# Attention loop: phases 0 and 1 of each chunk are multiplied with V in one block on TensorE, ahead of score tile 8

## The chip, the core and the metric

The kernel runs on one core of one Trainium2 chip. The metric is the device time of one execution in microseconds, median of several runs. The engines work from queues of their own and meet at semaphores: TensorE (PE, with its weight loads as PEld), VectorE (DVE), ScalarE (ACT), GpSimd (POOL) and SyncE (SP), which here only starts DMAs.

## What is computed

A gated cross-attention block and a mixture of experts, for 16 batches of 224 rows of width 512, with 750 context rows each:

```python
x = x + tanh(g_xattn) * xattn(layernorm(x), ctx, ctx, ctxb, ...)
x = x + tanh(g_ffn) * ffn(layernorm(x), ...)

# xattn, 16 heads of 32
Q, K, V = q_x @ Wq + bq, k_x @ Wk + bk, v_x @ Wv + bv        # split by head
scores = einsum('bhqd,bhkd->bhqk', Q, K) / sqrt(32)
scores = scores * gate[:, None, None, :]                     # from ctxb, 0.1 or 1
attn = softmax(scores)
out = einsum('bhqk,bhkd->bhqd', attn, V) ... @ Wo + bo
```

All is float32. The change touches the attention only.

## The kernel before

The attention is a loop over batches, with the first and the last batch written out of the same function `batch` and 14 passes of a loop between them. Each engine has its own order, written by hand. There is no scheduler: what stands ahead in an engine's code stands ahead in its queue.

A batch has four **chunks** c of four heads. A chunk has 12 **ticks** u = 0 to 11: in each, `score_columns` (L1155) makes one transposed score tile of 125 keys by 224 queries, twice, for one head, into one of two PSUM buffers `st`, and ScalarE's `exponential` (L613) turns it into `probs_t`. Tile u may be written once exponential u − 2 is done. Four ticks are a **phase**: phase 0 is ticks 0 to 3, phase 1 ticks 4 to 7, phase 2 ticks 8 to 11. `probs_t` holds two phases, so that exponential 8 needs phase 0 to have been read.

`attend(b, c, p)` (L1172) multiplies phase p with V: eight matmuls into the four 32-column strips of the array, a **block**. In the trace each shows as two records, so a block is x16. It waits for the last exponential of its phase, for p = 0 also for `normed`: VectorE's `normalize_output` of the chunk before, which reads and frees the tile `pv` and writes `out_t` (L869 to L871). `sum_up` (L1181) adds the sums of the exponentials behind phase 2, in the same 32-column form.

Between the ticks TensorE does other work:
- `next_scores(b, h, t)` (L1129), a score row of a head that comes 6 heads later, into the single tile `score`. Each needs VectorE's maximum (L848) of the row before. From h = 16 on it is a head of the next batch, and (16, 0), behind tile 6 of chunk 2, needs the stacked keys k_stack of that batch.
- `turn_shift` (L1143), a small transposition of the maxima, which ScalarE copies (L621), VectorE splits and ScalarE's DMA (L638) places in q_stack for the next chunk's or batch's tiles.
- the projections: V of the current and the next batch (L1103), K (L1093) and Q (L1081) of the next, the output projection of the last (L1116). They share three PSUM tiles `proj`; each is taken when its reader of three projections ago is done. The second half of Q takes the one that VectorE reads for q_lo (L831).

The keys of the next batch go this way: a half (K0a, K0b, ...) is projected on TensorE; VectorE gates it (`fresh`, L843); ScalarE makes the high part (`k_hi`, L583); GpSimd the low part (`k_lo`, L437); SyncE stores both (L301) and loads the stack (L317). In GpSimd's queue of chunk 1 the low part of K0b stands behind two additions (L482, L484) that need exponentials 8 and 9. In ScalarE's queue of chunk 1, `place_shift` (two DMA issues) and a normalisation (L602) stand between exponentials 8 and 9, and of chunk 2 the copy k_hi of K2a stands ahead of exponential 7.

V of the next batch goes from `proj` to `v_sb` by ScalarE's `copy_values` (L590). In chunk 3 ScalarE's code has:

```python
exponential(b, 3, u)
...
if not last and u == 6:
    copy_values(n, 0, b)        # n = b + 1
```

and `copy_values` waits until the old V tile has been read:

```python
act.wait_ge(pv_done, phases(n - 1, DC - 1, kt // 2) + 1)
```

which for tile 0 is phase 0 of chunk 3. Exponential 7 stands behind this copy.

## Time and profile before

| | |
|---|---|
| runs | 2049.89 us (2047.63 to 2052.6), 3 runs |
| profiled execution | 2065.15 us, its span 2063.2 |
| TensorE busy | 1948.6 us, 94% of the span |
| GpSimd, VectorE, ScalarE busy | 59%, 54%, 38% |
| attention loop | from about 78 to 1480 us, 15 batches of 88 us, the last 80 |
| granted TensorE clock | 0.969 over the span; 1.00 from 104 to 1421 us |

A share of busy time is an average; where an engine's queue is followed from record to record, the start of one to the start of the next is what it cost. A record of TensorE can overlap the next one. "[0.19 <-DVE out_t L871]" at a row's end is time without work ahead of it and what ended it. The rows below are mostly from the batch that begins at 694.45 us.

### The profile page before, as it was taken

The numbers are of one execution on the slowest core, as the hardware profiler recorded it, in microseconds if no ns is written. First come the engines' busy times: TensorE is split into PE (matmuls) and PEld (weight loads), VectorE is DVE, ScalarE is ACT, GpSimd is POOL, SyncE is SP. The second block draws the span as 40 slices with busy tenths as digits, with TensorE's granted clock in tenths as the row PEclk, the third lists the DMA queues.
The fourth block names the chain that finished last, engine by engine and source line by source line (L and its number), as shares of the span: only waits on it lengthen the run. The fifth ranks groups of instructions, "written<-read, shape, count | busy, mean of one in ns | idle before, by whom it ended". The sixth has DMA issues, their size and how long they took to land. (4 is left out here: it accounts for less than half of the span.)

```text
span 2063.2 us, 40622 instructions
## 1 busy us (share of the span) xinstructions
PE 1948.6 (94%) x12484; PEld 1510.4 (73%) x12485; DVE 1117.1 (54%) x1772; ACT 777.1 (38%) x1541; POOL 1226.6 (59%) x1391
## 2 busy tenths in 40 slices
PE   6799999999999999999999999998769999999899
PEld 5587877878777787877878777785458666666687
DVE  4565565655556555565665656555347333333576
ACT  3335444444544444444444544444222122221000
POOL 2367677776767777677776767766524333333352
PEclk9899999999999999999999999998579999999899
DMA  7754837457383654837557383664062554445675
GB/s 221 187 144 120 240 98 203 137 148 202 107 234 102 183 161 121 246 98 194 143 141 206 109 227 112 173 170 131 19 248 77 179 165 146 149 144 172 178 222 152
DMA packets 170571, 330.51 MB, mean 160 GB/s; under 512 B 20295, under 2 KB 69447, under 8 KB 169879
## 3 DMA queue, kind: packets, MB, share of 16 engines
q1 hardware_dynamic: 156700, 286.97, 49.3%
q0 software_dynamic: 10880, 33.56, 6.0%
q10 hardware_dynamic: 2944, 9.38, 1.2%
q8 instruction: 27, 0.44, 0.1%
q14 instruction: 20, 0.16, 0.0%
HBM read 214.17 MB, written 115.14 MB: 160 GB/s over the span
## 5 line engine op out<-in xcount | busy, mean ns | idle before, releaser
L848 DVE TENSOR_REDUCE neg_max<-score 112x1 f32<-112x750 f32 x512 | 480.7, 939 | 570.4 <-PE score L1129 569.3
L613 ACT ACTIVATE probs_t<-st 125x448 f32<-125x448 f32 x768 | 413.6, 542 | 514.9 <-PE st L1155 512.1
L482 POOL TENSOR_TENSOR acc<-acc,probs_t 125x448 f32<-125x448 f32 x256 | 309.5, 1209 | 66.1 <-ACT probs_t L613 64.3
L1155 PE MATMUL st<-q_stack,k_stack 98*125 98x224 f32 x1536 | 336.1, 302 | 5.0 <-ACT probs_t L613 2.7
L1093 PE MATMUL proj<-ctx_hi,weights 128*128 128x376 f32 (+1 forms) x1024 | 329.7, 347 | 0.0
L1155 PEld LDWEIGHTS st<-q_stack,k_stack 98*125 98x125 f32 x1536 | 269.0, 192 | 60.1 <-issue 28.3
L484 POOL TENSOR_TENSOR acc<-acc,probs_t 125x448 f32<-125x448 f32 x256 | 299.0, 1168 | 20.1
L1129 PE MATMUL score<-k_stack,q_stack 96*112 96x512 f32 (+1 forms) x1024 | 286.1, 361 | 23.8 <-DMA k_stack<-k_parts 12.4
L1103 PE MATMUL proj<-weights,ctx_hi 128*125 128x512 f32 x768 | 249.1, 406 | 5.0 <-issue 5.0
L474 POOL TENSOR_TENSOR acc<-probs_t 125x448 f32<-125x448 f32 x128 | 146.1, 1143 | 168.3 <-PE pv L1181 149.7
L1129 PEld LDWEIGHTS score<-k_stack,q_stack 96*112 96x112 f32 x1024 | 160.5, 179 | 80.7 <-issue 53.5
L1093 PEld LDWEIGHTS proj<-ctx_hi,weights 128*128 128x128 f32 x1024 | 192.4, 190 | 25.3 <-issue 16.1
L1172 PE MATMUL pv<-probs_t,v_sb 125*32 125x224 f32 x3072 | 191.9, 369 | 7.4 <-DVE out_t L871 6.6
L437 POOL TENSOR_TENSOR k_lo<-fresh,k_hi 128x376 fp32r<-128x376 f32 (+1 forms) x128 | 117.1, 915 | 97.3 <-ACT k_hi L583 97.3
L1093 PE MATMUL proj<-parts,weights 128*128 128x376 f32 (+1 forms) x512 | 172.1, 336 | 0.0
L2229 PE MATMUL gu_ps<-gu_sb,xg_t 128*128 x576 | 155.4, 398 | 4.0 <-DVE xg_t L2181 1.7
L2229 PEld LDWEIGHTS gu_ps<-gu_sb,xg_t 128*128 128x128 f32 x576 | 99.0, 191 | 78.4 <-issue 66.4
L1103 PE MATMUL proj<-weights,parts 128*125 128x512 f32 x384 | 152.5, 397 | 0.0
L1103 PEld LDWEIGHTS proj<-weights,ctx_hi 128*125 128x125 f32 x768 | 125.7, 189 | 34.6 <-issue 16.1
L1081 PE MATMUL proj<-xn_t,wq_sb 128*128 128x224 f32 x512 | 122.3, 364 | 12.4 <-DVE q_lo L831 10.3
L1116 PE MATMUL proj<-wo_sb,out_t 128*112 128x512 f32 x256 | 126.0, 607 | 0.0
L1172 PEld LDWEIGHTS pv<-probs_t,v_sb 125*32 125x32 f32 x3072 | 82.8, 111 | 55.9 <-DVE out_t L871 10.0
(212 smaller groups left out, 2758.3 us busy)
## 6 DMA issues: line engine op xcount, KB each, us to landing
k_stack<-k_parts SPq DMA_DIRECT2D x192, 375.0 KB, 6.2
ctx_raw<-in_ctx_t SPq DMA_DIRECT2D x64, 375.0 KB, 10.0
k_parts<-k_hi SPq DMA_DIRECT2D x64, 375.0 KB, 6.9
k_parts<-k_lo SPq DMA_DIRECT2D x64, 375.0 KB, 7.2
y_slots<-y_sb SPq DMA_DIRECT2D x72, 256.0 KB, 3.0
q_stack<-q_parts SPq DMA_DIRECT2D x64, 224.0 KB, 5.9
gu_sb<-in_w_gu ACTq DMA_DIRECT2D x4, 2048.0 KB, 15.6
x_in<-in_x SPq DMA_DIRECT2D x16, 448.0 KB, 9.2
```

Source lines behind the costliest of these rows:

```text
L474: nc.gpsimd.tensor_tensor(acc[0:KW, 2 * pair:2 * pair + 2, :], tiles(c, 0, pair, 0), tiles(c, 0, pair, 1), ALU.add).then_inc(added, 1)
L482: nc.gpsimd.tensor_tensor(both, both, tiles(c, p, pair, 0), ALU.add).then_inc(half_added, 1)
L484: nc.gpsimd.tensor_tensor(both, both, tiles(c, p, pair, 1), ALU.add).then_inc(added, 1)
L613: act.activation(probs_t[0:KW, (c * PHASES + p) % 2, u % HC, :], st[u % 2][0:KW, 0:2 * L], ACT.Exp)\
L848: nc.vector.tensor_reduce(neg_max[:, h // HC % 2, h % HC, t:t + 1], score[0:QW, 0:S], axis=AX.X, op=ALU.max, negate=True).then_inc(maxed, 1)
L1093: ins = nc.tensor.matmul(bank[:, 0:w], wp[:, d, c * P:(c + 1) * P], xp[:, d, at:at + w], start=(d == 0 and k == 0), stop=(d == DC - 1 and ...
L1103: ins = nc.tensor.matmul(bank[0:KW, :], xp[:, d, kt * KW:(kt + 1) * KW], wp[:, d, :], start=(d == 0 and k == 0), stop=(d == DC - 1 and k = ...
L1116: ins = nc.tensor.matmul(bank[0:QW, :], out_t[:, c, t * QW:(t + 1) * QW], wo_sb[:, c, :], start=(c == 0), stop=(c == DC - 1))
L1129: ins = nc.tensor.matmul(score[0:QW, at:at + w], q_stack[0:ROWS, h, t * QW:(t + 1) * QW], k_stack[0:ROWS, h, at:at + w], start=True, stop= ...
L1155: ins = nc.tensor.matmul(st[u % 2][0:KW, k * L:(k + 1) * L], k_stack[0:SHIFTED, h, kt * KW:(kt + 1) * KW], q_stack[0:SHIFTED, h, :], start ...
L1172: ins = nc.tensor.matmul(pv[j * DH:(j + 1) * DH, 0:L], v_sb[0:KW, kt, at:at + DH], probs_t[0:KW, (c * PHASES + p) % 2, j, k * L:(k + 1) * ...
L2229: ins = nc.tensor.matmul(gu_ps[k % 2][:, 0:GATE_UP], xg_t[:, k % 2, c, :], gu_sb[:, bass.ds(expert, 1), c, :].rearrange("p a m -> p (a m)" ...
```

## The change

In each chunk `attend` of phase 0 moves from behind tile 7 to directly ahead of tile 8, and `attend` of phase 1 from behind tile 10 to directly behind it. Phase 2 stays behind tile 3 of the next chunk. Nothing else is changed: no other engine's code, no buffer, no semaphore. The diff, cut to chunk 0 and chunk 3 (chunks 1 and 2 are changed in the same way; in chunk 2 there is no `turn_shift` ahead of the block, the score row (16, 1) stands there):

```diff
                 score_columns(b, 0, 7)
-                attend(b, 0, 0)
                 if not first:
                     project_out(b - 1, 0, b, (2, 3))
                 next_scores(b, 8, 1)
                 turn_shift(b, 1, b)
+                attend(b, 0, 0)
+                attend(b, 0, 1)
                 score_columns(b, 0, 8)
...
                 score_columns(b, 0, 10)
-                attend(b, 0, 1)
                 next_scores(b, 9, 1)
...
                 score_columns(b, 3, 7)
-                attend(b, 3, 0)
                 if not last:
                     project_v(1, b, (2, 3))
                 next_scores(b, 20, 1)
                 if not last:
                     turn_shift(n, 0, b)
+                attend(b, 3, 0)
+                attend(b, 3, 1)
                 score_columns(b, 3, 8)
...
                 score_columns(b, 3, 10)
-                attend(b, 3, 1)
                 if not last:
                     project_v(2, b, (2, 3))
```

What TensorE's queue holds in chunk 3 of the loop, from tile 7 to tile 8, before (st are tiles, pv blocks, proj with weights V projections, score a score row in two halves):

```order
L1155 MATMUL st<-q_stack,k_stack 125x224 x2
L1172 MATMUL pv<-probs_t,v_sb 32x224 x8
L1103 MATMUL proj<-weights,ctx_hi 125x512 x2
L1103 MATMUL proj<-weights,parts 125x512
L1126 REGISTER_ALU
L1129 MATMUL score<-k_stack,q_stack 112x512
L1129 MATMUL score<-k_stack,q_stack 112x238
L1043 REGISTER_ALU
L1143 MATMUL proj<-ident,neg_max 8x112
L1151 REGISTER_ALU
L1155 MATMUL st<-q_stack,k_stack 125x224 x2
```

and now:

```order
L1155 MATMUL st<-q_stack,k_stack 125x224 x2
L1103 MATMUL proj<-weights,ctx_hi 125x512 x2
L1103 MATMUL proj<-weights,parts 125x512
L1126 REGISTER_ALU
L1129 MATMUL score<-k_stack,q_stack 112x512
L1129 MATMUL score<-k_stack,q_stack 112x238
L1043 REGISTER_ALU
L1143 MATMUL proj<-ident,neg_max 8x112
L1172 MATMUL pv<-probs_t,v_sb 32x224 x8
L1167 REGISTER_ALU
L1172 MATMUL pv<-probs_t,v_sb 32x224 x8
L1151 REGISTER_ALU
```

The first block stands behind the transposition L1143 instead of directly behind tile 7, and the second, which stood behind tile 10, directly behind the first. In chunk 1 of the loop, TensorE's queue behind the transposition, now:

```order
L1143 MATMUL proj<-ident,neg_max 8x112
L1172 MATMUL pv<-probs_t,v_sb 32x224 x8
L1167 REGISTER_ALU
L1172 MATMUL pv<-probs_t,v_sb 32x224 x8
L1151 REGISTER_ALU
L1155 MATMUL st<-q_stack,k_stack 125x224 x2
L1093 MATMUL proj<-ctx_hi,weights 128x374
L1093 MATMUL proj<-parts,weights 128x374
L1093 MATMUL proj<-ctx_hi,weights 128x374
L1081 MATMUL proj<-xn_t,wq_sb 128x224 x2
L1155 MATMUL st<-q_stack,k_stack 125x224 x2
```

Both blocks stand ahead of tile 8, of the end of the K0b projection (L1093) and of the first two query projections (L1081); before, only the first block stood ahead of them, further up. The other four engines' queues are the same as before.

## Rows read from the trace of the kernel before

**Rows 1.** Waits of TensorE, whole run: engine line <- whom, us in total, times, longest

```profile
PE score L1129 <- DMA k_stack<-k_parts: 12.4, 15, 3.3
```

**Rows 2.** TensorE timeline, chunk 3: start, us, engine, line, operation, tiles, count

```profile
770.13 0.38 PE L1155 MATMUL st<-q_stack,k_stack 98*125 98x224 f32 x2
770.35 0.50 PE L1129 MATMUL score<-k_stack,q_stack 96*112 96x512 f32 x2
770.69 0.63 PE L1103 MATMUL proj<-weights,ctx_hi 128*125 128x512 f32 x2
...
771.38 0.37 PE L1155 MATMUL st<-q_stack,k_stack 98*125 98x224 f32 x2
771.69 0.96 PE L1172 MATMUL pv<-probs_t,v_sb 125*32 125x224 f32 x16
772.58 0.73 PE L1103 MATMUL proj<-weights,ctx_hi 128*125 128x512 f32 x2
...
773.38 0.50 PE L1129 MATMUL score<-k_stack,q_stack 96*112 96x512 f32 x2
...
773.75 0.46 PE L1155 MATMUL st<-q_stack,k_stack 98*125 98x224 f32 x2
774.04 0.63 PE L1103 MATMUL proj<-weights,ctx_hi 128*125 128x512 f32 x2
```

**Rows 3.** TensorE timeline, chunk 2: a block with the sums behind it

```profile
742.64 0.96 PE L1172 MATMUL pv<-probs_t,v_sb 125*32 125x224 f32 x16
743.42 0.56 PE L1181 MATMUL pv<-acc,ones_col 125*32 125x224 f32 x8
```

**Rows 4.** ScalarE timeline, chunk 3: the V copy and exponential 7

```profile
772.72 0.60 ACT L590 ACTIVATE v_sb<-proj 125x512 f32<-125x512 f32 x1 [1.55 <-PE pv L1172]
773.21 0.54 ACT L613 ACTIVATE probs_t<-st 125x448 f32<-125x448 f32 x1
```

**Rows 5.** TensorE timeline, chunk 1

```profile
727.18 0.38 PE L1155 MATMUL st<-q_stack,k_stack 98*125 98x224 f32 x2
727.74 0.96 PE L1172 MATMUL pv<-probs_t,v_sb 125*32 125x224 f32 x16 [0.19 <-DVE out_t L871]
...
729.25 0.50 PE L1129 MATMUL score<-k_stack,q_stack 96*112 96x512 f32 x2
...
730.13 0.46 PE L1155 MATMUL st<-q_stack,k_stack 98*125 98x224 f32 x2
...
731.80 1.02 PE L1081 MATMUL proj<-xn_t,wq_sb 128*128 128x224 f32 x4 [0.69 <-DVE q_lo L831]
```

**Rows 6.** VectorE timeline, chunks 0 and 1: the maxima behind out_t

```profile
706.65 0.94 DVE L848 TENSOR_REDUCE neg_max<-score 112x1 f32<-112x750 f32 x1
...
727.60 0.93 DVE L848 TENSOR_REDUCE neg_max<-score 112x1 f32<-112x750 f32 x1
```

**Rows 7.** ScalarE timeline, chunk 1: exponentials 8 and 9

```profile
731.05 0.52 ACT L613 ACTIVATE probs_t<-st 125x448 f32<-125x448 f32 x1
...
733.28 0.52 ACT L613 ACTIVATE probs_t<-st 125x448 f32<-125x448 f32 x1
```

**Rows 8.** GpSimd timeline, chunk 1: low part of K0b

```profile
736.30 0.98 POOL L437 TENSOR_TENSOR k_lo<-fresh,k_hi 128x374 fp32r<-128x374 f32 x1
```

**Rows 9.** TensorE timeline, chunk 2 of two batches: first score row of next batch

```profile
573.31 0.59 PE L1129 MATMUL score<-k_stack,q_stack 96*112 96x512 f32 x2 [1.18 <-DMA k_stack<-k_parts]
...
749.91 0.59 PE L1129 MATMUL score<-k_stack,q_stack 96*112 96x512 f32 x2 [0.74 <-DMA k_stack<-k_parts]
```

**Rows 10.** ScalarE timeline, chunk 2: exponential 7 behind a key copy

```profile
752.60 0.53 ACT L613 ACTIVATE probs_t<-st 125x448 f32<-125x448 f32 x1
```

**Rows 11.** TensorE timeline, chunk 0: tile 7

```profile
706.45 0.38 PE L1155 MATMUL st<-q_stack,k_stack 98*125 98x224 f32 x2
```

**Rows 12.** Stretches of the last batch: us, busy by engine, PEclk, DMA share, GB/s

```profile
1421.00:1431.60 10.60, 6.35 (x52) 4.27 (x50) 8.26 (x14) 7.28 (x12) 6.97 (x13) 1.00 0.14 44
1431.70:1469.00 37.30, 30.29 (x179) 19.35 (x179) 16.82 (x20) 15.34 (x31) 25.18 (x19) 0.50 0.10 30
```

More of the change, by code:

```diff
@@ L1316, in batch @@
                 score_columns(b, 1, 7)
-                attend(b, 1, 0)
                 if not last:
@@ L1323, in batch @@
                 turn_shift(b, 2, b)
+                attend(b, 1, 0)
+                attend(b, 1, 1)
                 score_columns(b, 1, 8)
@@ L1332, in batch @@
                 score_columns(b, 1, 10)
-                attend(b, 1, 1)
                 if not last:
@@ L1374, in batch @@
                 score_columns(b, 2, 7)
-                attend(b, 2, 0)
                 if not last:
@@ L1378, in batch @@
                 next_scores(b, 16, 1)
+                attend(b, 2, 0)
+                attend(b, 2, 1)
                 score_columns(b, 2, 8)
@@ L1389, in batch @@
                 score_columns(b, 2, 10)
-                attend(b, 2, 1)
                 if not last:
```

## The prediction

> **What bounds the kernel now.** I read the waits first. TensorE's longest waits inside the loop are those for the stacked keys (k_stack), 12.4 us over 15 times [rows 1]. Then the timelines of one pass of the loop (694.4 to 782.7 us, 88.3 us; the passes repeat to within some tens of ns, except for the k_stack wait). TensorE's records follow each other without a gap, so whatever adds or removes time in its queue counts in full, and a delay elsewhere counts only where TensorE meets it. So I take the four chunks one by one, and ask at each new place of a block whether its data are there. I call the block of eight matmuls of a phase p0 or p1 and count score tiles 0 to 11 of a chunk.
>
> **What a visit to the 32-column form costs.** In chunk 3, a tile followed by a score row takes 0.22 us (770.13 to 770.35), but tile 7, followed by a block, takes 0.31 (771.38 to 771.69); the three projection records after the block take 0.80 (772.58 to 773.38) where the same three take 0.69 elsewhere (770.69 to 771.38); and the block takes 0.89 (771.69 to 772.58) [rows 2]. A block followed by the sums, which have the same form, takes 0.78 [rows 3]. So a visit costs 0.09 in, 0.11 out and about 0.10 in the group behind it. Merging removes one visit, 0.30 us. In chunks 0, 1 and 3 the block now stands behind the small transposition L1143, which already makes the tile behind it take 0.29 (773.75 to 774.04) instead of 0.22; there both old visits' entries and exits go and one exit stays, 0.48 us saved: two entries of 0.09, two groups behind of 0.10, one exit of 0.11, less 0.02 because the tile behind the merged block takes 0.31, not 0.29. How a block starts directly behind L1143 isn't shown: between 0 and 0.09 (the entry from a tile); I take 0.04. In sum the switches give back 0.44 us in each of three chunks and 0.30 in chunk 2, 1.6 us a batch. The Trainium skill (TensorEngine Tiling (Array Packing), Key Properties) says that changing the tiling mode drains TensorE. The rows agree, with the prices above; by this rule alone the change is a gain (that is rival B).
>
> **Chunk 3: a wait in a ring.** ScalarE's queue has, in this order, exponential 6, the copy of V tile 0 of the next batch, exponential 7. The copy may not overwrite V before p0 of chunk 3 has read it: it starts at 772.72, 1.03 us after the block's start at 771.69, exponential 7 starts 0.49 later and takes 0.54 [rows 2, 4]. Today p1 comes far later. Now p1 follows p0 at once and needs exponential 7. From tile 7 (time 0): tile 0.22, projection 0.69, score row and L1143 0.37 (773.38 to 773.75), so p0 starts at 1.28 and p1 could start at 2.06. Exponential 7 ends at 1.28 + 1.03 + 0.49 + 0.54 = 3.34; with 0.07 for the handover (block's end 772.65 to copy 772.72) p1 starts at 3.41. That is a **new wait of 1.35 us**. p1 takes 0.89, tile 8 starts at 4.30; today at 2.37 (773.75 − 771.38). At its old place p1 goes with 0.09 + 0.89 + 0.10 = 1.08. Net 4.30 − 2.37 − 1.08 + 0.02 + 0.04 = **+0.91 us**. Behind the waiting block in TensorE's queue stand tile 8 and all that follows; ScalarE and VectorE idle behind it.
>
> **Chunk 1: one wait for another, and the keys later.** Today p0 waits for VectorE's out_t (tile 7 at 727.18, block at 727.74: 0.56 instead of 0.30). It now stands later and that wait goes, 0.26. But the score row behind it, which p0 covered, needs VectorE's maximum that starts at 727.60 and takes 0.93: it ends 1.35 after tile 7, with handover 1.42, while TensorE is there at 0.22 + 0.52 = 0.74. New wait 0.68. (Score row, three key projections and L1143 take 0.88, 729.25 to 730.13; less 0.37 for the first and last as in chunk 3, three key projections take 0.51 to 0.52.) Behind the wait come these 0.88, the blocks 0.78 + 0.89: tile 8 starts at 3.97, today at 2.95 (730.13): +1.02 [rows 5, 6]. Then the q_lo wait in front of the query projection (0.69, [rows 5]) disappears, since VectorE is earlier and TensorE later; and p1's old place gives 1.08 back. So TensorE is, after chunk 1, 0.74 us ahead of today. But exponential 8 waits for tile 8. It starts today at 731.05, 3.87 after tile 7, held up by ScalarE's own queue; now not before 3.97 + 0.53 (tile 8's 0.46 and a handover) to 4.60: 0.63 to 0.73 later, I take 0.68. Exponential 9 follows 2.23 behind, bound by ScalarE's queue (two DMA issues, a normalisation) [rows 7]; GpSimd's two additions for phase 2 need it, and in its queue stands behind them the low part k_lo of K0b [rows 8], then the store, the load, and the first score row of the next batch in chunk 2, which already waits 0.74 here [rows 9]. So that row comes 0.68 (+0.04) later although TensorE is there 0.7 earlier: **+0.72 us**, and the k_stack wait grows from 0.8 to about 2.2. Bounds: 0.4 if ScalarE catches up, 0.9 if exponential 9 waits for tile 9.
>
> **Chunk 2.** All runs from that score row, T = 749.91. Exponential 7 stands in ScalarE's queue behind a key copy that needs VectorE's gated keys: it starts at 752.60, ends T + 3.23, so p1 can start at T + 3.30 [rows 9, 10]. TensorE would be there after a score row (0.34, up to 0.1 more behind a wait; I take 0.42), key projections 0.52, tile 0.22, key projections 0.52, score row 0.34, entry 0.09 and p0 0.78: 2.89. Wait 0.4, visit −0.30: **+0.10**, between −0.30 and +0.2.
>
> **Chunk 0.** The visits give 0.48 less 0.04, and the out_t wait of 0.07 goes. Score row (8,1) loses the cover of p0: VectorE's maximum starts at 706.65 and takes 0.94, so ends 1.14 after tile 7 (706.45) [rows 6, 11]; handed over at 1.21. TensorE has only tile 7 and one output projection to do until then, which no row of mine prices; if they take no less than 0.65 together the wait is at most 0.55, and if they take more than 1.21 it is nothing. I take a quarter of the way, 0.13, and as much for row (9,1), which loses the cover of p1: **−0.25**, between −0.55 and +0.2. No DMA, and no instruction of another engine's queue, is moved.
>
> **Sum.** −0.25 + 0.72 + 0.10 + 0.91 = 1.48 us for a full batch, 14 of them 20.7. The first batch has chunks 1 to 3 alike, 1.5. The last has no projections and no V copy or key chain; there the merge may save or cost 1, I take 0. In all **+22 us**: on the profiled execution's 2065.15 (span 2063.2 and 1.95 around it) 2087; on the median of the runs, 2049.89, the same 22, so 2072.
>
> **Rivals.** *A, forecast:* both the ring and the later keys, 2072. *B, the switches win:* the visits come out as worked out, the waits don't: if ScalarE's copy doesn't stand in the way (wait 1.35 gone) and the keys land early enough, a batch changes by −0.25 − 0.70 + 0.10 − 0.44 = −1.3, some 2031. It needs both: with the ring in place (+0.91) the rest would have to fall below −0.91, and even with the keys on time it is −0.85; the ring's wait decides, from 1.3 us downwards. Against it speaks the order of ScalarE's queue, in which the copy at 772.72 waited 1.55 us for the block and the exponential followed it [rows 4]. *C, the keys have slack in the timed runs:* they are 15 us faster than the profiled one, and 12.4 us of that could be this wait. Where the load isn't late, TensorE keeps its 0.70 and a batch comes to −0.25 − 0.70 + 0.10 + 0.91 = +0.06: 2051. Partial slack gives all between 2051 and 2072. *D, the clock:* over 1421 to 1431.6 us TensorE was busy 6.35 of 10.6 us, split by short waits, and behind it the granted clock is 0.50, the lower of its two levels (1.2 GHz) [rows 12]. A wait of 2.2 us (up to 2.7, where it is 1.2 today, 573.31 in [rows 9]) in each of 15 batches could do the same. If it falls after half of them and costs 1 to 3 us each, +7 to +22: 2079 to 2094. Against it: around that wait of 1.2 us the granted clock stayed 1.00. *E, nothing moves:* the order shows the blocks merged in TensorE's queue, so it could only be that gains and waits cancel, 2050.
>
> **How the numbers follow.** A 0.56, D 0.22, C 0.12 (half of it within 0.2%, which is about what a measurement of this kernel can tell from no change), B 0.08, E 0.02. Forecast 2072. Range: down to most of C, up to the greater part of D: 2054 to 2093. Slower by over 0.2% (above 2054): 0.56 + 0.22 + 0.06 = 0.84, with the edge of C 0.85; same 0.07; faster 0.08.
>
> **What would show it.** In chunk 3, p0 and p1 apart by some 2.1 us, ended by ScalarE's probs_t, 15 times; ScalarE's copy of V between them. In chunk 1, no wait for out_t and q_lo, one of 0.7 for neg_max. The first next-batch score row waiting 2.2 us for k_stack instead of 0.8. The granted clock 1.00 in the loop (A) or with gaps (D). The forecast is wrong if p1 doesn't wait in chunk 3, if the keys' low part isn't later behind tile 7, or if the merged block takes other than 1.67 us without a wait.

## The result, and the profile after

| | before | after |
|---|---|---|
| median of the runs | 2049.12 us, 4 runs | 2114.3 us, 4 runs (2104.96 to 2117.06) |
| profiled execution | 2065.15 us, span 2063.2 | 2113.91 us, span 2112.0 |
| a batch of the loop, mean of 14 | 88.23 us | 92.56 us |

After over before is 1.0321 (95% interval 1.0297 to 1.0346): 65 us slower. Forecast were 2072 and a range that ended at 2093, so the direction was right and the size too small by 42 us. The loop accounts for the result: 14 × 4.34 = 60.7 us. The two profiled spans differ by 48.8 us only, because the one before had 12 us more between the start of its last batch and its end (663.2 us against 651.1). So the predicted 1.48 us a batch stand against 4.34.

TensorE's waits after, over the whole run (engine line <- whom it waited for: us in total, times, longest), answer to [rows 1]:

```profile
PE score L1129 <- DMA k_stack<-k_parts: 32.4, 15, 4.7
PE score L1129 <- DVE neg_max L848: 20.8, 33, 3.3
PE pv L1172 <- ACT probs_t L613: 18.3, 17, 1.2
PE st L1155 <- DMA q_stack<-shift_rows: 17.6, 16, 2.6
PE pv L1172 <- DVE out_t L871: 1.9, 2, 1.4
```

Three of the four large ones were predicted: the keys (12.4 us before; one of the 15, 4.7 now and 3.3 then, lies ahead of the first batch at 55 us, and the 14 of the loop average 1.98 us, 1.64 to 2.57, against 0.65 before), the maxima, and ScalarE's exponential in chunk 3 (1.15 us, about once a batch). The fourth was not. L1155 is the score tile, and what it waits for is the placing of the maxima (`place_shift`) into q_stack.

**Chunk 3**, TensorE and then ScalarE (start, us, engine, line, operation, tiles, count, idle time before and what ended it), answers to [rows 2, 4]:

```profile
799.77 0.38 PE L1155 MATMUL st<-q_stack,k_stack 98*125 98x224 f32 x2
...
801.03 0.26 PE L1143 MATMUL proj<-ident,neg_max 112*8 112x112 f32 x1
801.22 0.96 PE L1172 MATMUL pv<-probs_t,v_sb 125*32 125x224 f32 x16
803.34 0.96 PE L1172 MATMUL pv<-probs_t,v_sb 125*32 125x224 f32 x16 [1.15 <-ACT probs_t L613]
804.23 0.48 PE L1155 MATMUL st<-q_stack,k_stack 98*125 98x224 f32 x2
```
```profile
802.25 0.60 ACT L590 ACTIVATE v_sb<-proj 125x512 f32<-125x512 f32 x1 [2.70 <-PE pv L1172]
802.75 0.54 ACT L613 ACTIVATE probs_t<-st 125x448 f32<-125x448 f32 x1
```

The ring stands there as worked out: block, copy of V, exponential 7, block. The blocks start 2.12 us apart, forecast was 2.13 (3.41 − 1.28). Tile 7 to tile 8 takes 4.46 us, forecast was 4.30.

**Chunk 1**, TensorE, then the exponentials 8 and 9, then GpSimd's low part of K0b, answers to [rows 5, 7, 8]:

```profile
752.49 0.38 PE L1155 MATMUL st<-q_stack,k_stack 98*125 98x224 f32 x2
...
753.90 0.59 PE L1129 MATMUL score<-k_stack,q_stack 96*112 96x512 f32 x2 [0.51 <-DVE neg_max L848]
...
754.85 0.26 PE L1143 MATMUL proj<-ident,neg_max 112*8 112x112 f32 x1
755.04 1.72 PE L1172 MATMUL pv<-probs_t,v_sb 125*32 125x224 f32 x32
756.69 0.47 PE L1155 MATMUL st<-q_stack,k_stack 98*125 98x224 f32 x2
...
757.52 0.92 PE L1081 MATMUL proj<-xn_t,wq_sb 128*128 128x224 f32 x4
```
```profile
757.36 0.55 ACT L613 ACTIVATE probs_t<-st 125x448 f32<-125x448 f32 x1 [1.47 <-PE st L1155]
...
759.60 0.53 ACT L613 ACTIVATE probs_t<-st 125x448 f32<-125x448 f32 x1
```
```profile
762.63 0.99 POOL L437 TENSOR_TENSOR k_lo<-fresh,k_hi 128x374 fp32r<-128x374 f32 x1
```

Both old waits are gone, and 0.67 us are lost to the maximum (753.90 − 752.49 = 1.41 where 0.74 would do). Behind tile 7 the low part of K0b starts after 10.14 us, before after 9.12.

**Chunk 2**, TensorE, then three stretches (us, busy by engine with counts, granted TensorE clock, DMA share, GB/s), answers to [rows 9]:

```profile
773.29 0.38 PE L1155 MATMUL st<-q_stack,k_stack 98*125 98x224 f32 x2
775.68 0.60 PE L1129 MATMUL score<-k_stack,q_stack 96*112 96x512 f32 x2 [2.02 <-DMA k_stack<-k_parts]
...
776.88 0.60 PE L1155 MATMUL st<-q_stack,k_stack 98*125 98x224 f32 x2
...
779.00 2.06 PE L1172 MATMUL pv<-probs_t,v_sb 125*32 125x224 f32 x32
780.99 0.48 PE L1155 MATMUL st<-q_stack,k_stack 98*125 98x224 f32 x2
```
```profile
760.00:776.00 16.00, 13.98 (x102) 12.75 (x101) 9.17 (x13) 7.49 (x16) 11.64 (x11) 1.00 0.71 191
776.40:779.70 3.30, 3.30 (x18) 2.54 (x20) 1.97 (x3) 0.95 (x2) 1.14 (x2) 0.50 0.86 268
780.00:790.00 10.00, 8.83 (x76) 7.58 (x68) 4.26 (x8) 3.99 (x9) 6.40 (x7) 1.00 0.73 176
```

The wait of 2.02 us is the predicted one. Just behind it the granted clock is 0.50, 1.2 GHz, for 3.3 us, in which TensorE is busy throughout: tile 7 (776.88) shows 0.60 us where tile 6 (773.29) shows 0.38. The granted clock fell so in 13 of the 14 passes of the loop, and there the tick from tile 7 to tile 8 is 0.6 to 1.1 us longer than the 3.24 us that it takes at full clock. The loop's first pass is the exception. Its wait for the keys was 1.68 us, and the clock stayed at 1.00, where it fell behind one of 1.64 us in another pass; its tiles 7 and 8 on TensorE, and the two DMA issues that follow (of the maxima, and of the next stacked keys):

```profile
221.56 0.38 PE L1155 MATMUL st<-q_stack,k_stack 98*125 98x224 f32 x2
225.00 0.47 PE L1155 MATMUL st<-q_stack,k_stack 98*125 98x224 f32 x2
226.87 1.32 ACTq L638 DMA_DIRECT2D q_stack<-shift_rows  x2
228.96 1.30 SPq L317 DMA_DIRECT2D k_stack<-k_parts  x3
```

In this pass the tick took 3.44 us, tile 0 of chunk 3 did not wait for the maxima, and the sums behind tile 3 of chunk 3 waited 0.64 us for GpSimd instead.

**The first tile of chunk 3**, TensorE, ScalarE's queue (the DMA of the maxima) and SyncE's (the load of the next stacked keys, 3 × 375 KB):

```profile
786.40 0.55 PE L1058 MATMUL proj<-ident,x_res 112*128 112x112 f32 x4
788.12 0.47 PE L1155 MATMUL st<-q_stack,k_stack 98*125 98x224 f32 x2 [1.17 <-DMA q_stack<-shift_rows]
```
```profile
782.86 1.31 ACTq L638 DMA_DIRECT2D q_stack<-shift_rows  x2
```
```profile
783.43 1.57 SPq L317 DMA_DIRECT2D k_stack<-k_parts  x3
```

Before, this DMA was issued at 754.79 and the load at 757.44, 2.65 us apart, and the tile went at 759.75 without a wait. Now they are 0.57 us apart, and in the loop's first pass, where tile 0 did not wait, 2.09.

A batch from tick to tick (start of one score tile to the next, means of 14 batches, us against before), with what the prediction had for it:

| where | predicted | measured |
|---|---|---|
| chunk 0 | −0.25 | +0.02 |
| chunk 1, with the k_stack wait in chunk 2 | +0.72 | −0.80 + 1.53 = +0.73 |
| chunk 2, its merged block at full clock | +0.10 | +0.09 |
| chunk 2, tiles 7 to 8: the half clock | 0 (A), 1 to 3 in half the batches (D) | +0.85 |
| chunk 2 to 3: wait for the placed maxima | 0 | +1.32 |
| chunk 3, ticks 0 to 5: half clock in two batches, wait of the sums in one | 0 | +0.26 |
| chunk 3, merged block with the ring | +0.91 | +1.07 |
| sum | 1.48 | 4.34 |

The +0.85 is what that tick takes above the 1.08 which it gained where the same block ran at full clock (c2_only, below). The half clock has a share of the +1.53 too: at full clock the tick with the k_stack wait takes 1.32 us more than the wait itself, here 1.53 on average. So 1.33 of the 1.53 are the later keys and 0.20 the clock, which costs 1.05 us a batch in chunk 2 in all.

### The profile page after: what moved, and what is told of

The parts are those of the page before. It is cut to its first block and busy times, and to the rows that moved or that the text cites. A ratio compares the mean times of both kernels' runs of the same rounds, so it can differ in the third digit from the quotient of the medians.

```text
span 2112.0 us, 40622 instructions
## 1 busy us (share of the span) xinstructions
PE 1955.6 (93%) x12484; PEld 1515.2 (72%) x12485; DVE 1116.3 (53%) x1772; ACT 772.6 (37%) x1541; POOL 1226.7 (58%) x1391
## 5 line engine op out<-in xcount | busy, mean ns | idle before, releaser
L482 POOL TENSOR_TENSOR acc<-acc,probs_t 125x448 f32<-125x448 f32 x256 | 312.5, 1221 | 86.5 <-ACT probs_t L613 84.7
L1155 PE MATMUL st<-q_stack,k_stack 98*125 98x224 f32 x1536 | 341.8, 306 | 21.9 <-DMA q_stack<-shift_rows 17.6
L1155 PEld LDWEIGHTS st<-q_stack,k_stack 98*125 98x125 f32 x1536 | 271.7, 194 | 99.1 <-issue 65.9
L1129 PE MATMUL score<-k_stack,q_stack 96*112 96x512 f32 (+1 forms) x1024 | 287.9, 363 | 53.5 <-DMA k_stack<-k_parts 32.4
L1093 PE MATMUL proj<-ctx_hi,weights 128*128 128x376 f32 (+1 forms) x1024 | 332.9, 350 | 0.0
L484 POOL TENSOR_TENSOR acc<-acc,probs_t 125x448 f32<-125x448 f32 x256 | 307.6, 1202 | 20.1
L1129 PEld LDWEIGHTS score<-k_stack,q_stack 96*112 96x112 f32 x1024 | 160.5, 183 | 115.6 <-issue 59.1
L1172 PE MATMUL pv<-probs_t,v_sb 125*32 125x224 f32 x3072 | 186.7, 375 | 20.3 <-ACT probs_t L613 18.3
L1093 PEld LDWEIGHTS proj<-ctx_hi,weights 128*128 128x128 f32 x1024 | 197.8, 195 | 9.3
L1093 PE MATMUL proj<-parts,weights 128*128 128x376 f32 (+1 forms) x512 | 175.8, 343 | 0.0
L1172 PEld LDWEIGHTS pv<-probs_t,v_sb 125*32 125x32 f32 x3072 | 88.1, 114 | 87.5 <-issue 26.1
L1081 PE MATMUL proj<-xn_t,wq_sb 128*128 128x224 f32 x512 | 119.8, 360 | 1.2 <-DMA wq_sb<-in_wq 1.2
```

Source lines behind the costliest of these rows:

```text
L482: nc.gpsimd.tensor_tensor(both, both, tiles(c, p, pair, 0), ALU.add).then_inc(half_added, 1)
L484: nc.gpsimd.tensor_tensor(both, both, tiles(c, p, pair, 1), ALU.add).then_inc(added, 1)
L1093: ins = nc.tensor.matmul(bank[:, 0:w], wp[:, d, c * P:(c + 1) * P], xp[:, d, at:at + w], start=(d == 0 and k == 0), stop=(d == DC - 1 and ...
L1129: ins = nc.tensor.matmul(score[0:QW, at:at + w], q_stack[0:ROWS, h, t * QW:(t + 1) * QW], k_stack[0:ROWS, h, at:at + w], start=True, stop= ...
L1155: ins = nc.tensor.matmul(st[u % 2][0:KW, k * L:(k + 1) * L], k_stack[0:SHIFTED, h, kt * KW:(kt + 1) * KW], q_stack[0:SHIFTED, h, :], start ...
L1172: ins = nc.tensor.matmul(pv[j * DH:(j + 1) * DH, 0:L], v_sb[0:KW, kt, at:at + DH], probs_t[0:KW, (c * PHASES + p) % 2, j, k * L:(k + 1) * ...
```

## The experiments

All ratios are against the kernel before on the same chip; its median there was 2057.37 us for c1_only, c2_only, c3_only and ring_cut; 2058.2 for after_again, fill, pool_first and keys_early; 2063.65 for keys_chain, c2_sums, two_merged and all_remedied; 2049.25 for load_later and shift_behind. "A batch" is the mean of 14 in the profiled execution, against 88.23 us.

### The merge in one chunk alone, and without the ring

c1_only, c2_only and c3_only keep the merge in one chunk and leave the others as before. ring_cut is the changed kernel with the copy of V behind exponential 7:

```diff
-                    if not last and u == 6:
-                        copy_values(n, 0, b)
                     if not last and u == 7:
+                        copy_values(n, 0, b)
                         shift_high(n, 0, b)
```

**c1_only.**

> Only chunk 1 has the merged block; the other three chunks stand as before. Theory: tile 8, so exponentials 8 and 9, so GpSimd's low part of K0b, so the key stack come 0.7 us later while TensorE comes 0.8 us earlier. The first score row of the next batch waits 2.1 us for k_stack instead of 0.8, a batch costs +0.7 us for that. If this wait by itself makes the granted clock fall, as the changed kernel's profile suggests (one gap of 3.4 us a batch at 0.50 around it), another +0.8 to +1.1 us a batch: in all 2049 + 15 x 1.7 = about 2075, and the wait of tile 0 of chunk 3 for shift_rows stays near zero. Rival 1: the clock needs the other chunks' waits too: 2060, clock 1.00 in the loop. Rival 2: the shift_rows wait (1.3 us a batch in the changed kernel) comes from the late keys and not from chunk 2's merge: then it is here too, and the time is about 2090.

2071.77 us, 1.0069 (1.0042 to 1.0095). A batch +1.94: chunk 1 −0.80, the tick with the k_stack wait +1.62, and then +0.56 in the next and +0.37 ahead of tile 0 of chunk 3, which only some batches have: the tick behind the k_stack wait takes 3.4 to 3.9 us in 5 of 14 batches and 2.16 in the others, and the wait for q_stack<-shift_rows is there in three of these five and in no other. So the merge in chunk 1 alone brings the whole chain of keys, half clock and late maxima, in fewer batches. The profiled execution, 2085.96 us, is the slowest of the five; the 14 us at the median would be 1.0 a batch, if all of it lies in the loop.

**c2_only.**

> Only chunk 2 has the merged block. Theory: exponential 7 behind the key copy makes the second block wait 0.4 us, one visit of 0.3 is saved, +0.1 us a batch. Theory on the shift: tile 8 and exponential 8 come 1.1 us later, and with them the tiny DMA of the shift rows, which was issued 2.6 us ahead of the 1125 KB load of the next key stack and now meets it: tile 0 of chunk 3 waits for shift_rows, up to 1.3 us a batch: 2051 + up to 19, so about 2060 to 2070. Rival: the shift wait needs the half clock behind the long key wait, which delays tile 8 by another 0.8 us: then there is no such wait here and the time is 2050 to 2052. Clock in the loop 1.00 in both.

2082.61 us, 1.0121 (1.0093 to 1.015). Chunk 2 is even (−0.02, with 0.09 less of waiting for the keys), but the batch is 1.01 us longer: 0.84 of it is in tick 3 of chunk 3, where the sums of chunk 2 now wait for GpSimd. TensorE there:

```profile
771.13 0.96 PE L1172 MATMUL pv<-probs_t,v_sb 125*32 125x224 f32 x16
772.73 0.58 PE L1181 MATMUL pv<-acc,ones_col 125*32 125x224 f32 x8 [0.64 <-POOL acc L484]
```

Tile 8 of chunk 2 stands behind both blocks and comes 1.08 us later; exponentials 8 and 9 and GpSimd's four additions follow it, and there the delay isn't caught up. The prediction stopped at the end of chunk 2. In the changed kernel this wait shows in one batch of the loop alone, the one without the half clock: in the others TensorE loses more than that ahead of it to the half clock and the late maxima. The 14 × 1.01 us explain 14 of the 25 us by which the timed runs are slower; the rest isn't explained.

**c3_only.**

> Only chunk 3 has the merged block. Theory: the ring (first block, V copy, exponential 7, second block) makes the second block wait 1.36 us, switches give 0.3 back: +1.06 us a batch, 15 times: 2049 + 16 = 2065, k_stack wait and clock as before. Rival: without the other chunks' lateness ScalarE is early enough and the wait is gone: 2045.

2076.22 us, 1.0092 (1.0064 to 1.012); a batch +1.03, chunk 3 itself +1.08; 18.0 us over 16 times waited for probs_t, none in the loop for shift_rows. The ring alone costs what it costs in the changed kernel.

**ring_cut.**

> The changed kernel, with ScalarE's copy of V tile 0 moved from behind exponential 6 to behind exponential 7 in chunk 3, so that the second block no longer needs the copy. Theory: the block pair in chunk 3 takes 1.65 us instead of 3.01 in every batch, the time falls by 15 x 1.36 = 20 us from 2114 to about 2094. Rival: something else (the transposition and maxima behind it, or the V projections that wait for the copied tile) takes the wait over: the time falls by less than 8 us.

2090.71 us, 1.017 (1.014 to 1.0199). TensorE in chunk 3, from the transposition on (the code is one line shorter, so L1142 and L1171 are L1143 and L1172):

```profile
786.46 0.26 PE L1142 MATMUL proj<-ident,neg_max 112*8 112x112 f32 x1
786.65 1.72 PE L1171 MATMUL pv<-probs_t,v_sb 125*32 125x224 f32 x32
788.30 0.48 PE L1154 MATMUL st<-q_stack,k_stack 98*125 98x224 f32 x2
```

Tile 7 to 8 takes 3.10 us instead of 4.46: the ring's wait was 1.36 us, forecast 1.35. With it gone, chunk 3's merge gains 0.27 us. The half clock in chunk 2 now comes in 5 of 14 batches. Where it comes (tick of 4.4 us), the placed maxima are late by 0.6 to 1.2 us; where it doesn't (3.22, once 3.44), they are in time and the sums wait instead (0.83). So the two don't add: TensorE meets one or the other.

### What the half clock costs, and what brings it

after_again is the changed kernel again, on the chip of the others. fill puts nine matmuls, whose results are overwritten, into the wait for the keys:

```diff
                 score_columns(b, 2, 6)
+                if not last:
+                    pe.wait_ge(maxed, pieces(b, 16, 0))
+                    for _ in range(9):
+                        nc.tensor.matmul(score[:, 0:HALF_K[0]], wk_hi[:, 0, 0:P], ctx_hi[:, 0, 0:HALF_K[0]],
+                                         start=True, stop=True)
                 next_scores(b, 16, 0)
```

pool_first takes GpSimd's low part of K0b out of the queue behind the additions:

```diff
-                add_pair(b, 1, 2, 0)
                 if not last:
                     key_low(n, "K0b")
+                add_pair(b, 1, 2, 0)
```

**after_again.**

> The changed kernel once more, as the mark for the runs beside it on this chip. +4.3 us a batch and so 1.029 to 1.034 times the kernel before.

2117.37 us, 1.0298 (1.0266 to 1.0331); a batch +3.81, with the half clock behind the k_stack wait in 12 of 14 batches, and tile 0 of chunk 3 late in the same 12.

**fill.**

> The changed kernel, with nine extra 376-column matmuls (1.6 us, into the score tile, which the first score row of the next batch then overwrites) on TensorE ahead of its wait for k_stack in chunk 2. They lie inside the wait of 2.1 us and cost nothing. Theory: the fall of the granted clock in each batch comes from this wait, and the shift_rows wait of tile 0 of chunk 3 comes from the fall: the loop runs at clock 1.00, tick 7 of chunk 2 takes 3.2 us instead of 4.1, the shift_rows wait (1.3) goes and gives way to the wait of the sums for GpSimd (0.8, as with chunk 2's merge alone): 1.4 us less a batch, 20 us less than the changed kernel beside it. Rival 1: the shift_rows wait is the merge's own and stays: 12 us less. Rival 2: the clock falls for another reason: no change.

2116.55 us, 1.0294 (1.0266 to 1.0323): no gain in the timed runs, where 20 us were expected. In the profile the tick behind the filled wait takes 3.22 us and the wait for the placed maxima is gone from every batch, and still the batch gains only 0.64 us on after_again. What is late next are the sums (0.83, as in c2_only), and in 7 of 14 batches the half clock comes there. TensorE, and two stretches with the clock:

```profile
698.75 0.58 PE L1181 MATMUL pv<-acc,ones_col 125*32 125x224 f32 x8 [0.63 <-POOL acc L484]
...
700.71 0.87 PE L1066 MATMUL proj<-rw_sb,xn_t 128*112 128x16 f32 x8
701.43 1.07 PE L1103 MATMUL proj<-weights,ctx_hi 128*125 128x512 f32 x2
```
```profile
697.00:701.50 4.50, 3.87 (x48) 2.79 (x46) 1.01 (x2) 1.30 (x4) 3.59 (x5) 1.00 0.99 283
701.70:704.90 3.20, 3.20 (x10) 2.46 (x10) 1.31 (x4) 0.00 (x0) 0.87 (x1) 0.50 0.95 204
```

Ahead of the fall lie a wait of 0.63 us and matmuls of 16 columns; the same wait and matmuls stand in all 14 batches, and in 7 the clock stayed up. So with the half clock gone from chunk 2 the maxima's wait went too; and removing the fall in one place uncovers the next.

**pool_first.**

> The changed kernel, with GpSimd's low part of K0b moved ahead of the two additions that need exponentials 8 and 9. Theory: the low part is ready 0.9 us earlier, the key load starts up to 1.2 us earlier (then the q load ahead of it in SyncE's queue bounds it), the k_stack wait falls from 2.1 to about 1.0 us, the clock stays up in most batches, and with it the shift_rows wait goes: about 2.3 us less a batch, 30 to 35 us less than the changed kernel beside it. Rival: the load's landing is set by DMA traffic and not by its start: the wait stays at 2 us and the time changes by less than 5 us.

2097.35 us, 1.0192 (1.0164 to 1.0221), 20 us less than after_again. The k_stack tick is +0.41 instead of +1.29 (19.1 us of waiting over 16 times instead of 31.5), the tick behind it loses 0.08 to the half clock instead of 0.96 (it falls there in one batch), and the placed maxima are in time in the other 13; then the sums' wait (0.77) and some falls behind it take part of that back. So GpSimd's order of K0b is a cause of the whole chain in chunks 2 and 3, not a companion of it.

### Small transfer against large one

load_later is the changed kernel, with the load of the stacked keys of chunk 1 held back until tile 0 of chunk 3 is done:

```diff
                 sp.wait_ge(k_stored[c % 2], k_landed)
+                if keys_after is not None:
+                    sp.wait_ge(st_done, keys_after)
...
-                    load_stack(n, 1, ticks(b, 2, 0))
+                    load_stack(n, 1, ticks(b, 2, 0), ticks(b, 3, 1))
```

> The changed kernel, with SyncE's key load of chunk 1 of the next batch (three DMAs, 1125 KB) held until tile 0 of chunk 3 is done. Theory: tile 0 of chunk 3 waits for the small DMA of the shift rows because that is on its way at the same time as this load, which the half clock and the merge moved onto it; with the load held the shift wait of about 1.1 us a batch goes although the clock still falls, tick 11 of chunk 2 takes 1.6 us again, the wait of the sums for GpSimd takes back as much as 0.8 of it in tick 3 of chunk 3. In all 0.3 to 1.1 us less a batch, 4 to 16 us less than the changed kernel, 1.022 to 1.030 times before. Rival: the shift DMA is late by its own chain (exponential 8, two issues, another queue's load) and the wait stays over 0.8 us.

2106.53 us, 1.0277 (1.0258 to 1.0296); a batch +3.76. The half clock still fell in chunk 2 (tick up to 4.38 us), but tile 0 of chunk 3 waited in none of 14 batches. TensorE there, ScalarE's queue and SyncE's (L1061, L1158, L641 and L320 are L1058, L1155, L638 and L317):

```profile
785.97 0.55 PE L1061 MATMUL proj<-ident,x_res 112*128 112x112 f32 x4
786.28 0.46 PE L1158 MATMUL st<-q_stack,k_stack 98*125 98x224 f32 x2
```
```profile
782.41 1.30 ACTq L641 DMA_DIRECT2D q_stack<-shift_rows  x2
```
```profile
786.89 1.30 SPq L320 DMA_DIRECT2D k_stack<-k_parts  x3
```

The maxima's DMA is issued 3.87 us ahead of the tile, less than the 5.26 of the changed kernel, and is in time. So it wasn't issued too late; it landed late because 1125 KB of keys were loaded at the same time. The other profiles, the one before included, agree: counting in each of the 16 profiles the first batch and the 14 of the loop, tile 0 of chunk 3 waited for the maxima in all 41 batches in which the load was issued 0.93 us or less behind their DMA, and in none of the 199 in which it was 0.95 us or more. The first batch of c2_only is one of the 41, with 0.76 us between the two and a wait of 1.53 us, without late keys and at full clock: what counts is how near the two come, and the half clock is one way to it.

The whole gains little: tile 0 no longer waits, but the sums do (tick 3 of chunk 3 +0.83), and the k_stack wait is 0.2 us longer than in after_again (2.14 against 1.91; with the half clock in it, the tick is +1.73 against +1.29).

### The keys' chain, and versions meant to be faster

keys_early is the kernel before, with the K0b chain moved forward on VectorE, ScalarE and GpSimd and, for the first chunk, the load of the keys put ahead of the load of the queries in SyncE's queue. keys_chain is the same without SyncE's part (its edits on VectorE, ScalarE and GpSimd, in this order):

```diff
-                next_maximum(b, 13, 0)
                 if not last:
                     gate_keys(n, "K0b", b)
+                next_maximum(b, 13, 0)
...
                         place_shift(b, 2, b)
+                    if not last and u == 8:
+                        key_high(n, "K0b", b)
...
-                    if not last and u == 10:
-                        key_high(n, "K0b", b)
...
-                add_pair(b, 1, 2, 0)
                 if not last:
                     key_low(n, "K0b")
+                add_pair(b, 1, 2, 0)
```

**keys_early.**

> The kernel before (blocks at their old places), with the chain of K0b brought forward: VectorE gates it ahead of maximum (13,0), ScalarE makes its high part right behind the shift DMAs, GpSimd its low part ahead of the two additions, and SyncE starts the key load of chunk 0 ahead of its q load. Theory: the k_stack wait of 0.8 us, which is a real cost in the kernel before, goes: 15 x 0.8 = 11 us faster than before. Rival (C of the prediction, turned round): in the timed runs that wait is hardly there, and nothing is gained; or the work put ahead delays exponential 9 by 0.5 us and tile 11 waits for it: 0 to +5 us.

2076.83 us, 1.0092 (1.0061 to 1.0123): slower. The score row waits no longer for the keys but for the queries behind them, and longer than before (TensorE's waits; L1134 is L1129):

```profile
PE score L1134 <- DMA q_stack<-q_parts: 28.9, 16, 6.5
```

The small load of the queries behind the load of 1125 KB is finished later than the keys behind the queries were. The order of the two loads was right before.

**keys_chain.**

> The kernel before with the chain of K0b brought forward on VectorE, ScalarE and GpSimd as in the last try, but with SyncE's q load left ahead of its key load. Theory: the q load waits for the q store's landing (12.6 us after tile 7 of chunk 1 in every profile so far), so the key load starts at most 0.3 us earlier: -0.1 to -0.3 us a batch, 0 to -5 us, and the q_stack wait of the last try is gone. Rival: the earlier try's loss came from the moved work on ScalarE and VectorE and not from the order of the loads: again +10 to +20 us.

2062.36 us, 0.9999 (0.9983 to 1.0015), no difference; a batch −0.08. Moving the keys' chain forward brings nothing in the kernel before: the low part of K0b starts 3.2 us earlier behind tile 7 of chunk 1 (5.95 instead of 9.12), but the load of the queries, ahead of the keys in SyncE's queue, still starts at 12.7, and the load of the keys at 14.4 instead of 14.5.

**c2_sums** is c2_only with GpSimd's last two additions ahead of the low part of K3a:

```diff
                 add_pair(b, 2, 2, 0)
+                add_pair(b, 2, 2, 1)
                 if not last:
                     key_low(n, "K3a")
-
-                add_pair(b, 2, 2, 1)
```

> Chunk 2's merge alone, with GpSimd's low part of K3a moved from ahead of its last two additions for phase 2 of chunk 2 to behind them. Theory: chunk 2's merge makes exponentials 8 and 9 and so GpSimd's additions 1.1 us later, and the sums behind tile 3 of chunk 3 wait 0.83 us for them; the low part (0.85 us) out of the way, that wait goes, and a batch costs +0.1 to +0.2 instead of +1.01: 12 us less than chunk 2's merge alone, about +2 on the kernel before. Rival: the additions wait for the exponentials and not for the queue, so that the wait stays over 0.6: still +14 us.

2068.95 us, 1.0022 (1.0009 to 1.0034), against 1.0121 for c2_only. The sums' wait is gone (tick 39 of the batch 2.78 us instead of 3.58) and with it 0.87 of the 1.01 us of a batch. The rival, additions bound by the exponentials and not by the queue, is out. So the cost of merging in chunk 2 is that place in GpSimd's queue; and its gain, without the wait, is nothing.

**two_merged** merges in chunks 1 and 3 only, with ring_cut's and keys_chain's edits.

> Chunks 1 and 3 merged only, with the ring cut (V copy behind exponential 7) and the chain of K0b brought forward with SyncE's order as before. Theory: chunk 1 gives 0.80 and the keys are no later than before (bounded by the q load ahead of them), so the k_stack wait takes these 0.80 back: -0.1; chunk 3 -0.27: about -0.4 us a batch, 2 to 8 us faster than before. Rival: a k_stack wait of 1.6 us makes the clock fall in some batches and costs more than that: 5 to 15 us slower.

2046.04 us, 0.9917 (0.9896 to 0.9937): 0.8% faster than the kernel before. A batch −1.02: chunk 1 −0.80, the k_stack tick −0.02, chunk 3 −0.19. The score row of chunk 2 (L1128 is L1129):

```profile
739.18 0.59 PE L1128 MATMUL score<-k_stack,q_stack 96*112 96x512 f32 x2 [0.47 <-DMA k_stack<-k_parts]
```

TensorE keeps the 0.80 us that c1_only lost again to the keys, where the expectation had the wait for the keys take it back. Both loads come earlier with the merge: that of the queries starts 12.0 us behind tile 7 of chunk 1 instead of 12.7 in keys_chain, and that of the keys 13.7 instead of 14.4. The granted clock is 1.00 over the loop (104 to 1421 us), 0.98 in the changed kernel.

**all_remedied** is two_merged with the merge in chunks 0 and 2 too, and c2_sums' edit.

> The changed kernel (all four chunks merged) with all three orders mended: V copy behind exponential 7, the K0b chain forward, the low part of K3a behind the additions. Theory: of the +4.3 us a batch the ring takes 1.36, the keys about 1, clock and shift_rows wait about 1.2 (with the wait of the sums out of the way too) with them: -0.3 to +0.4 us a batch, within 6 us of the kernel before, clock 1.00 in most batches. Rival: a wait not yet seen takes over: more than 15 us slower.

2056.19 us, 0.996 (0.9941 to 0.9978); a batch −0.88. All four merges with all three queues mended are 0.4% faster than before, but chunks 0 and 2 add nothing: a batch is 0.13 us longer than in two_merged, and the timed runs 10 us slower, of which those batches explain 2.

**shift_behind** is two_merged with `turn_shift` behind the merged block in chunk 3:

```diff
                 next_scores(b, 20, 1)
-                if not last:
-                    turn_shift(n, 0, b)
                 attend(b, 3, 0)
                 attend(b, 3, 1)
+                if not last:
+                    turn_shift(n, 0, b)
                 score_columns(b, 3, 8)
```

> The mended kernel with chunks 1 and 3 merged, and in chunk 3 the transposition L1143 behind the pair of blocks instead of ahead of it. Theory: behind L1143 a block starts 0.16 us later than it could, while the entry from a score row costs 0.09, and L1143 ahead of the tile costs what the block's exit costs there: -0.1 us a batch against the kernel with two merged chunks, 0 to -2 us, hard to tell apart; 0.990 to 0.993 times before. Rival: the shift rows of the next batch come 1.7 us later and tile 0 of it waits: slower than that kernel by over 5 us.

2037.45 us, 0.9937 (0.992 to 0.9954); a batch −1.00. Tile 7 to 8 takes 3.03 us instead of 3.10. But the last tick of the chunk takes 0.12 more than in two_merged. It isn't told apart from two_merged.

## Why the prediction was right in its terms and wrong in its sum

Of the 2.86 us a batch between 1.48 and 4.34, 1.32 are the wait for the placed maxima and 1.05 the half clock in chunk 2. The sum had both at nothing: its path stopped at tile 8 of chunk 2, and rival D, the clock, was left out of the forecast. The rest is 0.26 behind these two in chunk 3, 0.27 in chunk 0 and 0.16 in the ring, less 0.2 in chunks 1 and 2.

- **Chunk 3's ring: right.** ring_cut puts the wait at 1.36 us (1.35 predicted). The term came out at 1.07 instead of 0.91, and the step that failed in it is "How a block starts directly behind L1143 isn't shown: between 0 and 0.09; I take 0.04": it starts 0.19 us behind the transposition (801.03 to 801.22), and the tile behind L1143 alone 0.03 (0.37 from score row to tile against 0.34 to L1143), so the entry costs 0.16, outside the bounds.
- **Chunk 1 and the keys: the mechanism right, the number in part luck.** The 0.67 us for the maximum, the lost waits for out_t and q_lo and the low part 1.0 us later came as worked out. But +0.73 against +0.72 holds 0.20 of half clock; the keys alone make it +0.53. Exponential 8 came 1.0 later, not 0.68: tile 8 starts 4.20 behind tile 7, not 3.97 (0.16 of it the entry). The load of the keys also started 1.0 us later behind tile 7 (15.54 against 14.52), but its last part landed only 0.5 later (23.03 against 22.51), which more than hid this. The 0.8 us of waiting before, from which the 2.2 was worked out, hold the wait of 3.3 us ahead of the first batch: in the loop it was 0.65 and became 1.98. Rival C, slack in the timed runs, is refuted: c1_only, which would be faster with it, is 0.7% slower in them.
- **Chunk 2's own term: right, its scope wrong.** "All runs from that score row" was followed to tile 8 and no further. That tile and the exponentials behind it are 1.08 us later there, as I had worked out for chunk 1; nobody was asked who waits for them. GpSimd's sums do (c2_only, +0.84), and c2_sums shows that it is they.
- **Chunk 0: wrong by 0.27 us.** The entry costs 0.12 more than taken, and the score rows wait some 0.3 and 0.2 us for their maxima instead of the 0.13 that I took for each: row (8, 1) starts 1.19 behind tile 7, close to the 1.21 of the handover, and tile 7 with its output projection leaves TensorE free after about 0.88 (0.22, and two matmuls of the kind of which four take 1.32 us in front of the tile at 730.77); the tick of row (9, 1) gives back 0.87 where chunk 2's gives 1.07. Above what was taken these are 0.12, 0.18 and 0.07, 0.37 in all; why the miss is 0.1 less isn't accounted for. The result stayed inside −0.55 to +0.2.
- **Rival D was real, and the forecast went without it.** Under "D, the clock" I gave 0.22 and a fall in half the batches at 1 to 3 us each. It fell in 13 of 14, behind the wait that I had forecast. Against it I had set that around the wait of 1.2 us in [rows 9] the clock stayed at 1.00; that row reached no further than 1.2 us, and the new waits were 1.64 to 2.57. Directly it costs 1.05 us a batch in chunk 2, about 15 us in all, which is within D's 7 to 22; with it the sum would have ended near 2087, inside the range, and the rest of the miss is mostly the term below.
- **The missing term.** The largest unpredicted item, 1.32 us, is tile 0 of chunk 3 waiting for the maxima. The step that failed is the prediction's own question, "ask at each new place of a block whether its data are there": it asked for the blocks and for the row that waited already, and not for the first tile of the next chunk. The sum followed the data through the engines' queues, and the DMAs only where one was late already. TensorE's delay in chunk 2 moved the maxima's small DMA, which depends on TensorE, against the load of the next keys, which depends on GpSimd. load_later shows the cause: with the load behind the tile the wait is gone in every batch of the loop. And where the half clock stayed away, in the first pass of the changed kernel, in 9 of 14 of ring_cut and in all 14 of fill, the two DMAs kept their distance and the wait stayed away too. The Trainium skill (DMA: Bandwidth & Descriptors, Issuing engines are not separate DMA queues) says that DMAs issued by different engines run on the same 16 DMA engines and interleave. The traces agree: with SyncE's load issued 0.57 us behind it, ScalarE's small DMA was not there after 5.26 us, and with that load held back it was there within 3.87.
- **Not settled.** When exactly the small DMA lands can't be read from this trace, only who waited. Fill's batch is 0.64 us shorter than after_again's in the profile, 9 us over the loop, but its first batch is 3.7 us longer (92.0 against 88.35) and the profiled span only 3.7 us shorter; the timed medians, 0.8 us apart with runs that spread over 12 us in each kernel, can't tell such a gain from none. Nor is it settled in which batches the clock falls: c1_only has k_stack waits at least as long (1.66 to 2.63 us) and fell in 5 of 14, ring_cut fell in 5, and there the ticks with the wait take 3.2 to 3.8 us in batches with a fall and 2.9 to 3.7 in the others. All falls in chunk 2 in the loops of all these kernels came behind a wait of 1.4 us or more (c2_only and c3_only, with at most 0.96 and 1.38, have none there), but the wait alone doesn't decide.

## What to carry to other kernels

A merge of like work on one engine gives back what the switches cost, and with it what waits it happens to remove or bring: here 0.2 us in chunk 3 and 0.8 in chunk 1, where two old waits went for one shorter new one, and nothing in the other two. It keeps that only where nobody waits for what now comes later: follow each delayed result through every other queue until it meets slack, across the end of the stage, with the DMAs that move against each other. A wait that grows beyond any in the trace before has to be priced with TensorE's clock behind it. A small DMA whose issue moves up to that of a large one has to be priced too. And such waits are in series: with one removed the next one takes over, so mend them together, and then merge only where the chunk alone gains.

## What the runs showed of the hardware that was not expected

- Waits of TensorE of 1.64 to 2.57 us between busy stretches were followed by a granted clock of 0.50, the lower level (1.2 GHz), in 13 of 14 batches of the changed kernel and, behind waits of 2.16 to 2.63, in 5 of 14 of c1_only, where one of 2.56 was not followed by it; the waits of 0.7 and 1.2 us of [rows 9] were not. In fill the clock fell behind a wait of 0.6 us with matmuls of 16 columns after it in 7 of 14 batches, in c2_only behind the same wait and matmuls in 2 of 14, in load_later in none. At 0.50 a score tile showed 0.60 us instead of 0.38.
- The 32-column block starts 0.19 us behind the start of an 8-column transposition, the tile in its place 0.03: the entry into the 32-column form costs 0.16 there against 0.09 from a tile. With block and transposition in the other order tile 7 to 8 took 0.07 us less.
- A small DMA from ScalarE, issued 0.57 us ahead of 1125 KB from SyncE, wasn't there 5.2 us after its issue began; with the load out of the way it was there within 3.9 us. Over all profiles the wait came with 0.93 us or less between the two issues, and never with 0.95 or more.
